# Recurrence of a delta-rule attention layer: selector products over 64 rows in alternating halves, two banks at a time, and a gram moved from leaf 9 to leaf 10

## The reference

```
def step(S, t):
    q_t, k_t, v_t, a_t, b_t = t
    y = einsum('bhvk,bhk->bhv', S, k_t)
    err = y - v_t
    S = a_t[..., None] * S - (b_t[..., None] * err)[..., None] * k_t[:, :, None, :]
    o = einsum('bhvk,bhk->bhv', S, q_t)
    return (S, o)
```

## Time and profile before

| | before |
|---|---|
| median of 3 runs (lowest to highest) | 3224.28 us (3220.03 to 3224.79) |
| the profiled execution, own time | 3222.9 us |
| its span in the profile | 3221.2 us |
| mean granted clock of TensorE | 0.976 |
| busy share of the span: PE, DVE, ACT, POOL | 90%, 72%, 50%, 41% |
| stretch 642 to 2782 us (the recurrence): PE, DVE, ACT, POOL busy | 1910, 1737, 1143, 893 of 2140 us |

### The profile page before, as it was taken

How to read it: one execution, slowest core, us unless ns; L and a number is a source line. 1 busy time by engine, 2 the same in 40 slices (tenths; PEclk the granted TensorE clock), 3 DMA queues, 4 the chain that set the end, 5 groups by cost and what they waited for, 6 DMA issues and landing times. The chain is left out here.

```text
span 3221.2 us, 48689 instructions
## 1 busy us (share of the span) xinstructions
PE 2896.1 (90%) x14232; PEld 2023.7 (63%) x14232; DVE 2324.0 (72%) x4837; ACT 1604.3 (50%) x3516; POOL 1319.6 (41%) x1577
## 2 busy tenths in 40 slices
PE   7999999678889898998989989898898988879999
PEld 3555555466667676776767767677676776635555
DVE  6777777678887888878887787887888788533322
ACT  6666666445555555555554555555555555321110
POOL 3667676634434444344443444434444344300000
PEclk9999999789999999999999999999999999889999
DMA  3556655722223221232322223222222221030000
GB/s 137 232 203 242 241 209 222 218 40 47 40 42 67 41 55 40 42 67 41 55 40 42 57 52 55 40 42 57 51 55 40 42 50 32 16 108 20 7 7 7
DMA packets 443035, 249.62 MB, mean 77 GB/s; under 512 B 401488, under 2 KB 413488, under 8 KB 440624
## 3 DMA queue, kind: packets, MB, share of 16 engines
q1 hardware_dynamic: 442816, 246.90, 28.8%
HBM read 141.88 MB, written 104.99 MB: 77 GB/s over the span
## 5 line engine op out<-in xcount | busy, mean ns | idle before, releaser
L265 DVE SCALAR_TENSOR_TENSOR A_acc<-A_psY,A_w,A_acc 128x410 f32<-128x410 f32 (+1 forms) x720 | 419.3, 637 | 151.6 <-ACT A_acc L334 151.6
L1155 ACT ACTIVATE B_WL<-B_psT 64x128 f32<-64x128 f32 (+3 forms) x480 | 148.3, 309 | 513.8 <-PE B_psT L1576 513.8
L840 POOL TENSOR_TENSOR B_WT<-B_WT,B_G 128x128 f32<-128x128 f32 (+2 forms) x224 | 182.3, 814 | 513.3 <-PE B_psT L1576 493.8
L405 PE MATMUL A_psY<-A_xT,A_w 128*128 128x413 f32 (+1 forms) x960 | 347.2, 510 | 9.1 <-PE A_psAG L411 7.7
L192 POOL TENSOR_TENSOR A_outs<-A_outs,A_acc 128x410 f32<-128x410 f32 (+1 forms) x240 | 229.4, 985 | 215.8 <-ACT A_outs L342 215.8
L1068 DVE TENSOR_TENSOR B_NC<-B_NC,B_psM 128x256 f32<-128x256 f32 x480 | 198.9, 414 | 144.6 <-PE B_psM L1603 102.0
L405 PEld LDWEIGHTS A_psY<-A_xT,A_w 128*128 128x128 f32 x960 | 180.2, 189 | 165.5 <-issue 164.2
L822 POOL TENSOR_TENSOR B_PQ<-B_PQ,B_G 128x256 f32<-128x256 f32 x128 | 125.7, 982 | 369.0 <-DVE B_WT L1036 369.0
L1071 DVE TENSOR_REDUCE B_W<-B_NC 128x64 f32<-128x320 f32 x512 | 248.7, 486 | 17.6
L1603 PE MATMUL B_psM<-B_BD,B_WL 128*128 128x128 f32 x1536 | 237.6, 296 | 12.6
L334 ACT ACTIVATE A_acc<-A_psY,A_w 128x410 f32<-128x410 f32 (+1 forms) x240 | 166.0, 692 | 163.2 <-PE A_psY L405 161.4
(11 more groups left out here) (201 smaller groups left out, 6859.2 us busy)
## 6 DMA issues: line engine op xcount, KB each, us to landing
B_KQ<-scr SPq DMA_DIRECT2D x96, 512.0 KB, 6.6
scr<-A_outs SPq DMA_DIRECT2D x48, 615.0 KB, 3.5
scr<-A_outag SPq DMA_DIRECT2D x32, 615.0 KB, 5.2
scr<-A_outs SPq DMA_DIRECT2D x48, 409.0 KB, 2.5
A_xc<-nbeta SPq DMA_DIRECT2D x16, 1024.0 KB, 5.9
B_A<-scr SPq DMA_DIRECT2D x32, 512.0 KB, 4.8
B_C<-scr SPq DMA_DIRECT2D x32, 512.0 KB, 5.9
B_G<-scr SPq DMA_DIRECT2D x32, 512.0 KB, 4.6
```

The source lines that it names most:

```text
L265: nc.vector.scalar_tensor_tensor(a, y, w[:, s, col:col + 1], a, ALU.mult, ALU.add)\
L405: last = nc.tensor.matmul(psY[p][:, y0:y0 + HALO + t1 - t0], wp[:, p, kt, :], xT[:, kt, t0:t1 + HALO], start=kt == 0, stop=kt == KT - 1)
L840: tt(dst, dst, gr, ALU.mult).then_inc(wsc.sem, 1)
L1155: copy = lambda out, in_: nc.scalar.activation(out, in_, ACT.Copy)
```

## The change

Three things change, all in the recurrence.

1. kk and qk run over 64 rows: each product takes only the half in which its leaf lies. Products for the even and the odd leaf alternate, and each leaf has a bank of its own. qk is three jobs of two banks in place of five of one: the first after leaf 0 (as much as two before), the second and third both after leaf 3. DVE makes three y terms in place of five (1024, 1024 and 512 elements), the first in leaf 1, the other two in leaf 4. ACT and DVE read kk from both banks at once. The four products of each pair of update jobs alternate between halves too.
2. Banks are no longer n mod 5. A table takes the bank that was given out longest ago, and for kk and qk the two neighbouring banks for which that is longest ago.
3. gram 5 moves from the head of leaf 9's jobs to behind kk in leaf 10's, and its mask from leaf 10 to leaf 11, ahead of `row_pairs`.

```diff
@@ def leaf_jobs(g, j):
-    jobs = {0: out and [("qk", 0), ("qk", 1)],
+    jobs = {0: out and [("qk", 0, 0), ("qk", 0, 1)],
             1: [("own", 1, 0), ("own", 1, 1)],
-            2: [("ktok", 0), ("gram", 1)] + (out and [("qk", 2)] or []),
-            3: out and [("qk", 3), ("qk", 4)],
+            2: [("ktok", 0), ("gram", 1)],
+            3: out and [("qk", 1, 0), ("qk", 1, 1), ("qk", 2, 0), ("qk", 2, 1)],
             4: [("kk", 1, 0), ("kk", 1, 1), ("gram", 4)],
...
-            9: [("gram", 5), ("decay", 0), ("decay", 1)],
-            10: [] if last else [("kk", 0, 0), ("kk", 0, 1)],
+            9: [("decay", 0), ("decay", 1)],
+            10: ([] if last else [("kk", 0, 0), ("kk", 0, 1)]) + [("gram", 5)],
...
-OUT_ROWS = [((0, 0, 2),), ((1, 1, 2),), ((2, 2, 2),), ((3, 3, 1), (0, 2, 1)), ((1, 3, 1), (0, 3, 1))]
+OUT_ROWS = [((0, 0, 2), (1, 1, 2)), ((2, 2, 2), (3, 3, 1), (0, 2, 1)), ((1, 3, 1), (0, 3, 1))]
+KEY_ROWS = ((0, 1, 3), (1, 2, 2), (2, 3, 1))
@@ def recurrence(...)
         for n, job in enumerate(JOBS):
-            seen[n % RING] += 1
-            place[job] = (n % RING, seen[n % RING])
+            if job in place:
+                continue
+            if job[1] in ("kk", "qk"):
+                first = min(range(RING - 1), key=lambda b: max(held[b][0], held[b + 1][0]))
+                place_in(first, n)
+                place_in(first + 1, n + 1)
+            else:
+                place_in(min(range(RING), key=lambda b: held[b][0]), n)
@@ def y_terms(o, n):
                 wait(dve, wxc, o, 1)
-                wait(dve, awm, o, (4, 5, 3, 6, 6)[n])
-                ps = take_bank(dve, o + 1, "qk", n)
-                x = WX[:, 2 * n:2 * n + 2]
-                tt(x, ps[:].rearrange("p (n c) -> p n c", n=2), x, ALU.mult).then_inc(yv.sem, 1)
+                wait(dve, awm, o, (5, 6, 6)[n])
+                m = 4 if n < 2 else 2
+                ps = take_two_banks(dve, o + 1, "qk", n)[:, :, 0:m * HJ2]
+                x = WX[:, 4 * n:4 * n + m].rearrange("p k (l x) -> p l k x", l=2)
+                tt(x, ps.rearrange("p l (k x) -> p l k x", k=m), x, ALU.mult).then_inc(yv.sem, 1)
@@ def row_pairs(i):
-                wait(dve, nlc, i, 1)
-                ps = rows(take_bank(dve, g if h else g - 1, "kk", h, 0))
-                tt(n[:, :, :, :, 11], ps[:, 1], a[:, 1], ALU.mult).then_inc(nl.sem, 1)
-                tt(n[:, :, :, :, 16], ps[:, 2], rr, ALU.mult).then_inc(nl.sem, 1)
                 wait(dve, nlc, i, 2)
-                ps = rows(take_bank(dve, g if h else g - 1, "kk", h, 1))
-                tt(as_rows(X[:])[:, 1], ps[:, 1], a[:, 2], ALU.mult).then_inc(nl.sem, 1)
+                ps = take_two_banks(dve, g if h else g - 1, "kk", h)
+                row = lambda k: ps[:, :, HJ2 // 2 * k:HJ2 // 2 * (k + 1)].rearrange("p l (h n) -> p l h n", h=H)
+                tt(n[:, :, :, :, 11], row(1), a[:, 1], ALU.mult).then_inc(nl.sem, 1)
+                tt(n[:, :, :, :, 16], row(2), rr, ALU.mult).then_inc(nl.sem, 1)
+                tt(as_rows(X[:])[:, 1], row(4), a[:, 2], ALU.mult).then_inc(nl.sem, 1)
@@ DVE's chunk(g)
                     elif j == 10:
-                        mask_gram(g, 5)
                         decay_state(g, 0)
                         decay_state(g, 1)
-                    elif j == 11 and more:
-                        row_pairs(nxt)
-                        leaf_solution(nxt, 1, 2)
+                    elif j == 11:
+                        mask_gram(g, 5)
+                        if more:
+                            row_pairs(nxt)
+                            leaf_solution(nxt, 1, 2)
@@ PE
+            def row_scalars(g, kind, n):
...
+                for k, (r, t0, m) in enumerate(runs):
+                    for leaf in range(2):
+                        p = slice(64 * leaf, 64 * leaf + 64)
+                        c = R * leaf + r
+                        last = mm(ps[:, leaf, at * width:(at + m) * width].rearrange("p (t x) -> p t x", t=m),
+                                  source[p, c:c + 1].to_broadcast([64, 128]),
+                                  rows[p, R * leaf + t0:R * leaf + t0 + m], start=True, stop=True)
...
+            def updates(g, half):
+
+                opened = [open_bank(pe, g, "update", 2 * half + r) for r in range(2)]
...
+                for m in range(4):
+                    i = 4 * half + m
+                    for r, (ps, filled) in enumerate(opened):
+                        p = slice(64 * r, 64 * r + 64)
+                        last = mm(ps[:, 128 * m:128 * (m + 1)], KTOK[p, i, :], WTOK[p, i, :], start=True, stop=True)
```

More of the change, by code:

```diff
@@ L541, in recurrence @@
         att = sb("att", [128, HID])
-        ring = [ctx.enter_context(nc.psum_tensor(f"B_ring{i}", [128, 512], FP32)) for i in range(RING)]
+        banks = ctx.enter_context(nc.psum_tensor("B_ring", [128, RING, 512], FP32))
+        ring = [banks[:, i] for i in range(RING)]
         psT = ctx.enter_context(nc.psum_tensor("B_psT", [128, 512], FP32))
@@ L632, in take_bank, with two_banks, take_two_banks @@
             return ring[b]
+        def two_banks(*job):
+            b, _ = place[(*job, 0)]
+            return banks[:, b:b + 2]
+        def take_two_banks(eng, *job):
+            for leaf in range(2):
+                b, k = place[(*job, leaf)]
+                eng.wait_ge(full[b], k)
+            return two_banks(*job)
         FQ = SQ[:].rearrange("p h c -> p (h c)")
@@ L1146, in _ @@
                 chunk(g)
-            for n in range(5):
+            for n in range(3):
                 y_terms(NCH - 1, n)
@@ L1460, in shared_job @@
                                   KQ[:, gi % 2, 1:3, :, r0:r0 + 2 * R], start=True, stop=True)
[L1461 to L1472, removed]
-                                      rows[:, R * leaf + t0:R * leaf + t0 + m], start=True, stop=True)
-                        at += m
                 elif kind == "gram":
@@ L1533, in shared_job @@
                         last = mm(ps[:, 0:HID], OG[:, h, :], wo[:, h, :], start=i == 0, stop=i == H // 2 - 1)
-                elif kind == "update":
-                    wait(pe, wtok, g, n // 2 + 1)
-                    wait(pe, ktok, g, 2)
-                    r = slice(64 * (n % 2), 64 * (n % 2) + 64)
-                    for m in range(4):
-                        i = 4 * (n // 2) + m
-                        last = mm(ps[:, 128 * m:128 * (m + 1)], KTOK[r, i, :], WTOK[r, i, :], start=True, stop=True)
@@ L1542, in shared_job @@
-                last.then_inc(filled, 1)
+                last.then_inc(filled, 1)
+            def row_scalars(g, kind, n):
+                if kind == "qk":
+                    rows, runs, width = QS[:, (g - 1) % 2].rearrange("p t h n -> p t (h n)"), OUT_ROWS[n], HJ2
+                else:
+                    rows, runs, width = KS[:], KEY_ROWS, HJ2 // 2
+                filled = [open_bank(pe, g, kind, n, leaf)[1] for leaf in range(2)]
+                if kind == "qk":
+                    wait(pe, qs, 2 * (g - 1) + 1, 1)
+                else:
+                    wait(pe, ks, 2 * g + (1 if n else 2), 1)
+                ps = two_banks(g, kind, n)
+                at = 0
+                for k, (r, t0, m) in enumerate(runs):
+                    for leaf in range(2):
+                        p = slice(64 * leaf, 64 * leaf + 64)
[3 more added lines that the diff above has]
+                                  rows[p, R * leaf + t0:R * leaf + t0 + m], start=True, stop=True)
+                        if k == len(runs) - 1:
+                            last.then_inc(filled[leaf], 1)
+                    at += m
@@ new lines, in updates @@
+            def updates(g, half):
+                opened = [open_bank(pe, g, "update", 2 * half + r) for r in range(2)]
+                wait(pe, wtok, g, half + 1)
+                wait(pe, ktok, g, 2)
+                for m in range(4):
[3 more added lines that the diff above has]
+                        last = mm(ps[:, 128 * m:128 * (m + 1)], KTOK[p, i, :], WTOK[p, i, :], start=True, stop=True)
+                        if m == 3:
+                            last.then_inc(filled, 1)
@@ L1544, in centered_rest, with run_job @@
+            def run_job(g, job):
+                if job[0] in ("kk", "qk"):
+                    if job[-1] == 0:
+                        row_scalars(g, job[0], job[1])
+                elif job[0] == "update":
+                    if job[-1] % 2 == 0:
+                        updates(g, job[-1] // 2)
+                else:
+                    shared_job(g, job)
             def centered_rest(g):
@@ L1554, in chunk @@
                 for i in range(4):
-                    shared_job(g, ("contact", i))
+                    run_job(g, ("contact", i))
                 for i in (2, 3):
-                    shared_job(g, ("gram", i))
+                    run_job(g, ("gram", i))
                 for j in range(J):
```

57 lines of the change are left out of this document (29 added, 28 removed).

## The result

| | before | changed |
|---|---|---|
| median (lowest to highest) | 3222.16 us (3215.67 to 3224.79, 4 runs) | 3246.28 us (3240.39 to 3251.19, 4 runs) |
| profiled execution: own time, span | 3222.9, 3221.2 us | 3240.4, 3238.6 us |
| mean granted clock | 0.976 | 0.958 |
| chunks 2 to 30 with a fall of the clock (a stretch at 0.50), in the profiled execution | 6 of 29 | 28 of 29 |

The ratio is 1.0074, 95% interval 1.0053 to 1.0095: 24 us slower, where 3253 was forecast.

A forecast was written before the change was run, and what follows sets the result against it. The recurrence, two thirds of the span, was taken to be bound leaf by leaf by DVE or late PE work, with the clock deciding. Profiled 3222.9 - 15.6 savings + 46 for clock falls = 3253 us, range 3207 to 3284.

The forecast's parts named there:

- savings of 15.6: Whole kernel at equal clock: -0.44 us a chunk over 31 chunks, about -2 for last y terms and first kk; -5 to -22.
- 20 more falls: Thinner PE stretch in leaves 9 and 10: clock falls in 27 of 31 chunks, not 7; +46 us (0 to +75).
- Leaf 0 to 1: Shorter qk lets leaf 1's transpose start earlier and a y term fit before DVE's product: -0.38 us a chunk.
- Leaves 3 to 5: Third y term enters full leaf 4, which grows 0.5 us, against a shorter kk: +0.12 us (-0.2 to +0.4).
- Leaves 9 to 12: Moved gram and mask: leaf 10 gains 0.60 us, given back waiting for the later mask: 0 (-0.3 to +0.2).
- Update: State update's halves alternate, so contact starts earlier at the chunk's end: -0.18 us a chunk (-0.2 to 0).
- Overlap: Alternating 64-row halves take 0.5 of the time: qk about 1.1 us, kk about 1.0, update about 2.0.
- rival 1: Clock in the recurrence: no more falls, the savings remain; 3207 us, chance 0.16.
- Rival 2: Clock in the recurrence: only some more falls, 10 to 17 in all; about 3222 us, chance 0.13.
- rival 3: Recurrence leaves: halves overlap no more than the update shows, new waits bite, no more falls; 3232 us, chance 0.05.

The follow-up runs named there:

- run 6: Kernel before, with leaf 9's decay transposes issued twice and, in even chunks, leaf 13's twice: 3208.62 us, ratio 0.9947 to the kernel before.
- run 5: Changed kernel, with leaf 9's decay transposes issued three times and, in even chunks, leaf 13's twice: 3181.91 us, ratio 0.9868 to the kernel before.
- run 1: Changed kernel, with leaf 9's eight decay transposes issued three times (16 more): 3196.98 us, ratio 0.9911 to the kernel before.
- run 11: Changed kernel, with 16 more decay transposes in leaf 13 of even chunks and none in leaf 9: 3241.69 us, ratio 1.0046 to the kernel before.
- run 12: Changed kernel, with gram 5 back in leaf 9, its mask in leaf 10, and leaf 9's decay transposes twice: 3224.21 us, ratio 0.9995 to the kernel before.
- run 4: Kernel before, with only the move of gram 5 and its mask; kk, qk and update over 128 rows: 3267.94 us, ratio 1.0170 to the kernel before.
- run 8: Changed kernel filled as in run 5, with key and output products' halves issued in blocks, not in turn: 3213.74 us, ratio 0.9972 to the kernel before.
- run 2: Kernel before, with leaf 9's eight decay transposes issued twice (8 more): 3236.59 us, ratio 1.0034 to the kernel before.

## Why the prediction was right

It said slower by 30 us, from savings of 15.6 and 20 more falls at 2.3 us. Measured: savings of 27 (run 6 less run 5), 22 more falls, and 24 us slower. The mechanism held. The nearness of the number is in part luck: the savings were 11 us larger than forecast and the falls cost about 5 us more, which pulls the other way. And 27 falls was a choice between the ends 7 and 31, not worked out.

- **The clock decided, as forecast.** Falls in 28 of chunks 2 to 30 and in chunk 1, so 29 of 31 (27 were forecast), beginning at 37.9 us already, behind an idle time of 1.98 us. A chunk with a fall is 2.0 us (even) or 2.7 us (odd) longer than one at full clock (66.2 and 70.5 against 64.16 and 67.77 in run 5); 2.3 was the forecast. As a whole the clock costs the changed kernel 64 us (3246.28 - 3181.91) and the one before 14 to 16; the difference of about 50 stands against the +46 of the sum. Runs 1, 5 and 11 show the cause: the loss goes when that stretch is filled and stays when another is.
- **Leaf 0 to 1:** -0.37 us for -0.38.
- **Leaves 3 to 5:** -0.24 for +0.12, the largest error. Leaf 4 grew 0.51 as said. But leaf 5 shrank 0.75: DVE waits 0.19 us for both kk copies, where it had waited 0.37 for one, and the 0.27 us that DVE waited for PE before leaf 6's product is gone. Over 31 chunks that is 11 us; the errors of the other leaves, below, nearly cancel.
- **Leaves 9 to 12:** 0 was forecast. At equal clock leaf 10 gains 0.60 and leaf 11 gives back 0.68. Of the 0.68, 0.30 comes with the new kk even without the move (3.56 in run 12), the rest with the gram's mask. What the sum lacked is leaf 13 of odd chunks, 5.06 for 5.46. There DVE's next product waits for PE to get through wo, and wo ends 4.06 us after leaf 13's first product in run 5, 4.46 in run 6: a delay of DVE in leaf 11 that PE doesn't share is won back here. The move is not needed for it (5.18 in run 12), and by itself it does nearly as much (5.07 in run 4). In the changed kernel without a fill no odd chunk had this gain: all fell, and leaf 13 lasted 5.46, which is 0.4 of the 2.7 us. Run 4 also shows when the move pays: behind a kk of full length it costs 0.5 us an odd chunk (69.27 for 68.76), behind the short one it gains 0.3.
- **Update:** -0.05 for -0.18. Its length and contact's distance came as forecast (2.55 us for 2.71), but the update starts 0.15 us later behind ACT's copy than before: in the trace 0.24 us pass between ACT's signal and the first product, for 0.09 before. PE's queue passes further waits in that time, for signals that had come 0.7 us or more earlier. That these waits cost the 0.15 us fits the trace; no run tests it.
- **Overlap:** kk 0.99 (1.0 forecast), qk 1.19 (1.1), update 2.06 (2.0). Taking 0.5 for full alternation was right for the products in turns. In blocks (run 8) it holds for the first qk group, but not for kk.

With the measured savings, rival 1 (no more falls) would be 3222.9 - 27 = 3196 us; run 1, with seven falls, came to 3197. Rival 2 falls with the 28 falls, rival 3 with run 5.

The Trainium skill's page TensorEngine Tiling (section Key Properties and Gotcha 1) says that the row halves of the array work at the same time if they write different PSUM banks; run 5 against run 8 agrees (1.13 against 1.57 us) for products issued in turns. No run here has both halves write to one bank. Its page TensorE: Matmul & The Clock Gate (section Why this matters for your kernels) blames whole idle gaps, longer than any here; 28 falls behind gaps of 1.98 us and 22 behind 1.74 disagree, since the clock fell without such a gap. The same page (section Part 4: PE-mode transpose) says that transposes don't count as work for the clock as products do; the 16 more transposes of run 1, which the trace writes as MATMUL, took 21 of 28 falls away, so here they did.

## What to carry to other kernels

Before taking PE work out of a stretch, look at the granted clock next to it: a stretch that passes at full clock only just is worth more full than short, and useless transposes there can pay (here 49 us for 16 in each chunk; 16 in leaf 13 of the even chunks took one fall of 28 away). After each such repair read where the falls went, since the next thin place may cost more. Compare two versions at equal clock before judging either: by the medians this change loses 24 us, at equal clock it gains 27, and with the fill and one y term moved it ends 1.8% below the kernel before.

## What was not expected of the hardware

- A fall pushed on can be dearer: 6.8 us at 0.50 from the end of leaf 10 on cost 2.3 us in an even chunk of the kernel before, 13.7 us at 0.50 from 54 us on cost 5.4 (run 2).
- Products of different jobs overlap if they are of different halves: in run 5 the first kk product starts at 1073.48, 0.01 us after the ring's own 64-row product, and ahead of that product's second pass. In blocks kk starts 0.32 us after it. And the order of issue is not kept: the ring's product lies in the first half, kk's first product too, yet in run 5 the kk products of the second half, each issued behind its neighbour, are by their signals done first in leaf 10, in each of chunks 3 to 29 (in run 8 in none of them).
- In neither kernel did a fall in chunks 2 to 30 need PE to be idle for more than 1.98 us at a time (before the change 1.11).
